# The early shared expert of a two-layer AdaLN kernel: whole blocks of 512 columns in place of halves, and another buffer

## What is computed

```python
h = _layernorm(x) * (1 + cb) + sb          # hidden, 2048 x 128
shared = _silu(hidden @ shared_gate_w.T) * (hidden @ shared_up_w.T) @ shared_down_w.T
x = x + gb * (shared + expert_sum)         # shared_gate_w, shared_up_w: 512 x 128
```

## Time and profile before

| | |
|---|---|
| three runs | 1034.47 to 1039.31 us, median 1035.91 |
| profiled execution | 1037.88 us |
| its span on the core | 1036.2 us |
| TensorE clock granted, mean | 0.959 of full speed |
| steps with the pieces of chunk 0 | about 257 to 374 us of the span |
| steps with the pieces of chunk 1 | about 414 to 531 us of the span |

### The profile page before, as it was taken

One profiled execution on the slowest core, in us unless ns is written; L12 is line 12 of the kernel. 1 busy time (PEld: TensorE's weight loads), 2 busy tenths in 40 slices (PEclk: granted clock), 3 DMA queues, 4 the chain that ended last, 5 costly groups with the idle time before them and its releaser, 6 DMA issues.

```text
span 1036.2 us, 23043 instructions
## 1 busy us (share of the span) xinstructions
PE 955.9 (92%) x9214; PEld 360.0 (35%) x9214; DVE 888.1 (86%) x1321; ACT 810.6 (78%) x1627; POOL 220.6 (21%) x395
## 2 busy tenths in 40 slices
PE   5999999999999999999999889979989998888888
PEld 2552322232333333333333235524323463232224
DVE  7989999999999998999998888854787877899804
ACT  4139999998999998999997678857864576667886
POOL 4233200003221203221112500051132212201112
PEclk9879999999999998999998889989997999999999
DMA  3510400000000000000000164112100441100000
GB/s 103 171 54 2 132 24 10 8 2 2 1 2 2 2 2 2 2 2 2 2 2 1 49 179 132 32 31 73 38 3 1 123 119 36 47 12 2 1 12 11
DMA packets 41387, 37.05 MB, mean 36 GB/s; under 512 B 5084, under 2 KB 39452, under 8 KB 41280
## 3 DMA queue, kind: packets, MB, share of 16 engines
q1 hardware_dynamic: 39024, 30.20, 10.1%
q0 software_dynamic: 1824, 5.25, 1.8%
q10 hardware_dynamic: 432, 0.13, 0.1%
HBM read 21.92 MB, written 13.30 MB: 34 GB/s over the span
## 4 chain that ended last, share of the span: by engine, by line
PE 52%; DVE 31%; issue 7%; ACT 6%; POOL 2%; DMA 1%; another core or an unknown queue 1%; ACTq 0%; POOLq 0%; DVEq 0%; SPq 0%
DVE mx L1374 25%; PE O L1057 19%; PE T L1022 11%; ACT PT L1631 2%; PE T L1136 2%; PE S L995 2%; PE T L1033 2%; PE T L1146 2%; PE S L987 2%; DVE S L1370 1%; ACT PT L1625 1%; PE S L1179 1%; POOL XP L1990 1%; PE O L914 1%; PE S L1128 1%
## 5 line engine op out<-in xcount | busy, mean ns | idle before, releaser
L1374 DVE TENSOR_REDUCE mx<-S 128x2 f32<-128x1024 f32 x608 | 705.7, 1220 | 38.8 <-PE S L987 20.5
L1631 ACT ACTIVATE PT<-T 128x512 f32<-128x512 f32 (+2 forms) x1280 | 657.4, 586 | 99.7 <-PE T L1033 43.2
L1057 PE MATMUL O<-PT,Va 128*9 128x256 f32 (+1 forms) x4040 | 335.5, 393 | 4.5 <-ACT Os L1665 4.5
L1022 PE MATMUL T<-Qs,Ks 26*128 26x512 f16 x1024 | 242.3, 392 | 12.1 <-ACT PT L1631 8.8
L987 PE MATMUL S<-Ks,Qs 24*128 24x512 f16 x1024 | 204.1, 398 | 7.7 <-DVE mx L1374 5.8
L1022 PEld LDWEIGHTS T<-Qs,Ks 26*128 26x128 f16 x1024 | 67.8, 91 | 229.9 <-issue 127.0
L1057 PEld LDWEIGHTS O<-PT,Va 128*9 128x9 f32 x4040 | 67.6, 88 | 125.9 <-issue 112.1
L1057 PE MATMUL O<-PT,V 128*17 128x256 f32 (+2 forms) x984 | 84.6, 414 | 1.4 <-ACT Os L1665 0.7
L995 PE MATMUL S<-K,Qs 48*128 48x512 f16 (+3 forms) x320 | 61.0, 363 | 17.1 <-DVE mx L1374 12.0
L1370 DVE CUSTOM_DVE_ANT_0 S<-S,gates 128x128 f32<-128x128 f32 (+3 forms) x128 | 59.7, 519 | 6.1 <-PE S L995 5.9
L987 PEld LDWEIGHTS S<-Ks,Qs 24*128 24x128 f16 x1024 | 48.2, 91 | 30.9 <-DVE mx L1374 23.7
(11 more groups left out here) (335 smaller groups left out, 894.2 us busy)
## 6 DMA issues: line engine op xcount, KB each, us to landing
Wg<-in_L_ffn_experts SPq DMA_DIRECT2D x28, 192.0 KB, 2.6
Ks<-in_L_ffn_experts SPq DMA_DIRECT2D x20, 192.0 KB, 2.6
Vf<-sorted_x SPq DMA_DIRECT2D x12, 256.0 KB, 4.6
sorted_y<-Vf SPq DMA_DIRECT2D x12, 256.0 KB, 2.3
rows_q<-q SPq DMA_DIRECT2D x7, 256.0 KB, 2.4
sorted_x<-XP POOLq DMA_DIRECT2D x1, 1792.0 KB, 10.7
Qs<-nrow SPq DMA_DIRECT2D x96, 2.0 KB
Qs<-rows_q SPq DMA_DIRECT2D x8, 192.0 KB, 3.7
```

Source lines behind the costliest of these rows:

```text
L1022: e.matmul(bank, Ks[r0:r0 + 26, quad, keys], Qs[r0:r0 + 26, quad, CH * c:CH * c + CH], start=True, stop=True, tile_position=(r0, 0)).then_ ...
L1057: m = e.matmul(acc[32 * g:32 * g + d1, lo:hi], v, PT[(2 * j + g // 2) % 4][:, p0 + lo:p0 + hi], start=fresh, stop=True, skip_group_check=n ...
L1374: e.tensor_reduce(mx[:, u % 2, h0:h0 + 2, kb], two[:, :, 0:n], AX.X, ALU.max).then_inc(free, 1)
L1631: e.activation(PT[(2 * j + pair) % 4][:, CH * i + lo:CH * i + CH], bank[:, lo:CH], ACT.Exp).then_inc(free, 1)
```

## The change

The gate and lift products of chunks 0 and 1 are made for all 512 rows of the chunk at once: 4 gates and 4 lifts for a chunk in place of 8 and 8. The four `lower` pieces stand together at the end in place of two after each half. There are 12 pieces for a chunk in place of 20, and they stand 4.2 steps apart in place of 2.5, so that they cover about the same steps. The buffer `gates` is now 3x512 columns in the last 1536 columns of `Vf`, and `triangle` has a tensor of its own. POOL's product of the second chunk waits for the first chunk's last `lower`.

```diff
@@ -244,10 +244,9 @@
             P.piece[a] = len(P.piece) + 1
             beside("gate", *a)
         pieces = []
-        for half in range(2):
-            for bl in range(4):
-                pieces += [lambda a=(c, bl, half): gate(*a), lambda a=(c, bl, half): beside("lift", *a)]
-            pieces += [lambda j=j: beside("lower", c, j) for j in (2 * half, 2 * half + 1)]
+        for bl in range(4):
+            pieces += [lambda a=(c, bl): gate(*a), lambda a=(c, bl): beside("lift", *a)]
+        pieces += [lambda j=j: beside("lower", c, j) for j in range(4)]
         for i, piece in enumerate(pieces):
             at(s + int(i * apart), piece)
 
@@ -295,7 +294,7 @@
             mix(t, c)
         elif c < 2:
             route(t + 5, c)
-            shared_pieces(t + 10, c, 2.5)
+            shared_pieces(t + 10, c, 4.2)
         elif c == 2:
 
             route(t + 2, 2)
@@ -680,7 +679,6 @@
         onesf = sb("onesf", [128, 128])
         wqT, wkT, wvT, woT = (sb(n, [128, 128]) for n in ("wqT", "wkT", "wvT", "woT"))
         bq, bk, bqs, bks, bv = (sb(n, [128, 1]) for n in ("bq", "bk", "bqs", "bks", "bv"))
-        gates = sb("gates", [128, 3, 256])
         bvb, boB, bpB = (sb(n, [128, 128]) for n in ("bvb", "boB", "bpB"))
         rwT = sb("rwT", [128, 16])
         XP = sb("XP", [128, 16, 128])
@@ -715,6 +713,7 @@
         rk = sb("rk", [128, 208])
         rt = sb("rt", [128, 12, 16])
         lg, eq, wv_ = (rt[:, 4 * i:4 * i + 4, :] for i in range(3))
+        vector_mask = sb("vector_mask", [128, CH], BF16)
         lm = sb("lm", [128, 16])
         wm = sb("wm", [128, 4])
 
@@ -738,7 +737,8 @@
         XS = Vf[:, 0:3584].rearrange("p (i n) -> p i n", n=128)
         ams = [Vf[:, 3584 + CH * i:3584 + CH * i + CH] for i in range(4)]
         bsg, bt = Vf[:, 5632:5632 + CH], Vf[:, 6144:6144 + CH]
-        triangle = gates[:, 0, :].bitcast(BF16)
+        gates = Vf[:, 6656:8192].rearrange("p (k n) -> p k n", k=3)
+        triangle = vector_mask[:, :]
         pick = Vf[:, 0:256].bitcast(F16).rearrange("p (k s m) -> p k s m", k=2, s=2)
         hS, tS, acS = ([Vf[:, 6656 + 512 * k + 256 * i:6656 + 512 * k + 256 * i + 256] for i in range(2)] for k in range(3))
         Kf = Ks[:, :, :].rearrange("p a n -> p (a n)")
@@ -1128,20 +1128,20 @@
                     e.matmul(two[:, 0, :], sgT[:, 128 * bl:128 * bl + 128], hc(c), start=True, stop=True).then_inc(gate_made, 1)
                     e.matmul(two[:, 1, :], suT[:, 128 * bl:128 * bl + 128], hc(c), start=True, stop=True).then_inc(full, 1)
                 elif name in ("gate", "lift"):
-                    c, bl, half = a
+                    c, bl = a
                     done(("turn", 1, c))
                     pe.wait_ge(ld_w1, LD_W1)
-                    bank, full = opened((name, c, bl, half))
+                    bank, full = opened((name, c, bl))
                     w = sgT if name == "gate" else suT
-                    e.matmul(bank[:, 0:256], w[:, 128 * bl:128 * bl + 128], hc(c, 256 * half, 256 * half + 256), start=True, stop=True).then_inc(full, 1)
+                    e.matmul(bank, w[:, 128 * bl:128 * bl + 128], hc(c), start=True, stop=True).then_inc(full, 1)
                 elif name == "lower":
                     c, j = a
                     bank, full = opened(("lower", c, j))
                     pe.wait_ge(po_scaled, SCALED["dn"])
-                    if (c, 3, 0) in P.piece:
-                        pe.wait_ge(gated, P.piece[c, 3, j // 2])
+                    if (c, 3) in P.piece:
+                        pe.wait_ge(gated, P.piece[c, 3])
                     for bl in range(4):
-                        if (c, 3, 0) not in P.piece:
+                        if (c, 3) not in P.piece:
                             done(("up", c, bl))
                         m = e.matmul(bank[:, 0:128], ams[bl][:, 128 * j:128 * j + 128], sdT[:, bl, :], start=bl == 0, stop=bl == 3)
                     m.then_inc(full, 1)
@@ -1710,11 +1710,11 @@
                     bank, free = filled((name,) + tuple(a))
                     if P.piece[tuple(a)] > 1:
                         ac.wait_ge(gated, P.piece[tuple(a)] - 1)
-                    e.activation(gates[:, 0, :], bank[:, 0:256], ACT.Tanh, scale=0.5)
-                    e.activation(gates[:, 1, :], bank[:, 0:256], ACT.Copy).then_inc(free, 1)
+                    e.activation(gates[:, 0, :], bank, ACT.Tanh, scale=0.5)
+                    e.activation(gates[:, 1, :], bank, ACT.Copy).then_inc(free, 1)
                 elif name == "lift":
                     bank, free = filled((name,) + tuple(a))
-                    e.activation(gates[:, 2, :], bank[:, 0:256], ACT.Copy).then_inc(free, 1)
+                    e.activation(gates[:, 2, :], bank, ACT.Copy).then_inc(free, 1)
                 elif name == "m0":
                     g, p = a
                     bank, free = filled(("m0", g, p))
@@ -1965,16 +1965,16 @@
                     po.settle()
                     e.tensor_tensor(hv, hv, sv.unsqueeze(2).to_broadcast([128, 4, 128]), ALU.mult).then_inc(prepared, 1)
                 elif name == "lift":
-                    c, bl, half = a
+                    c, bl = a
                     tanh, gate, lift = (gates[:, i, :] for i in range(3))
-                    done(("lift", c, bl, half))
+                    done(("lift", c, bl))
                     if c:
-                        passed(("lower", c - 1, 2 * half + 1))
+                        passed(("lower", c - 1, 3))
                     po.tick(e.tensor_tensor(tanh, tanh, gate, ALU.mult))
                     po.settle()
                     po.tick(e.tensor_tensor(tanh, tanh, gate, ALU.add))
                     po.settle()
-                    e.tensor_tensor(ams[bl][:, 256 * half:256 * half + 256], tanh, lift, ALU.mult).then_inc(gated, 1)
+                    e.tensor_tensor(ams[bl], tanh, lift, ALU.mult).then_inc(gated, 1)
                 elif name == "scatter":
                     g, t = a
                     po.wait_ge(positions, g + 1)
```

## The result

The changed kernel was slower: a median of 1042.98 us in 9 runs (1035.99 to 1047.91) beside 1034.81 us for the kernel before (1027.35 to 1042.14, 9 runs). The medians are 8.2 us apart. The ratio of the two sets of runs is 1.0092, with a 95% interval of 1.0065 to 1.0119, so 6.7 to 12.3 us more. Forecast was 1042.1 us from a median of 1035.91, that is +6.2. Its profiled execution took 1042.35 us, with a span of 1040.6.

A forecast was written before the change was run, and what follows sets the result against it. DVE was taken to set the pace without slack in layer 0's units; gates, lifts, first gate, collisions and POOL's wait sum to 6.9 us a chunk against 3.8, +6.2 for two, giving 1042.1 us from 1035.91, range 1034 to 1048.

The forecast's parts named there:

- DVE sets the pace: Layer 0 units: DVE has no slack; wide pieces delay its `s` tile, 0.82 us a gate, 0.35 to 0.4 a lift.
- POOL's queue ahead of `neg_turn`: Second lift: longer POOL operations delay the negated maxima's split; PE stands still about 1.5 us, costing 1.2 us a chunk.
- The sum: Units 5 to 7 and the first gate: 6.9 us a chunk in place of 3.8, +3.1; two chunks +6.2.
- the first gate: Gate behind DVE's six routing operations: only PE's longer product counts, 0.35 us a chunk.
- collisions: Units 5 to 7: pieces near `o_turn`, `neg_turn` or each other; 1.3 us a chunk, where narrow ones cost 2.0.
- down projections: Four a chunk, at steps 15, 3, 8 and 13 of a unit: keep their 2.2 us, 0.55 each on average.
- The clock: Units with wide pieces: PE's longer stops lower its clock from 2.4 to 1.2 GHz, time passes 1048 us; 8 in 100.
- Width doesn't matter: Rival: a wide piece costs about its two narrow ones, only POOL's wait remains; 1036 to 1039 us, 34 in 100.
- Instructions count, not columns: Rival: each insertion costs DVE 0.27 us whatever its width, so 16 fewer make it faster; 1030.1 us, 10 in 100.
- The Trainium skill's rule: ACT: two 256-column ACTIVATEs cost 93 ns more than one of 512, saving 2.2 us, off the path where DVE is full.

The follow-up runs named there:

- the kernel with the slower POOL: Kernel before, narrow pieces kept, POOL doing two more 256-column products in one lift per chunk ahead of the negated maxima's split; ratio to before 1.0049 (1.0013 to 1.0085).
- the quarters: Kernel before with pieces of 128 rows: 16 gates and 16 lifts a chunk, 1.35 steps apart, one `lower` per quarter; ratio to before 1.0098 (1.0065 to 1.0131).
- the side work behind the `s` tile: Side work of steps 78 to 191 placed after its half step's `s` tile in PE's order; ratio to before 1.0128 on the changed kernel, 1.0057 on the kernel before.

## Why the prediction was right, and where it was short

- *DVE sets the pace, and the loss is in its gaps.* Shown: 0.88 us at a calm wide gate and 0.39 at a calm wide lift, in DVE's own rows. The sum had 0.82 (2.5 for three) and 0.35 to 0.4, from shifting the narrow gate's rows by 0.4 for PE and 0.42 for ACT; the `s` tile moved by 0.86.
- *POOL's queue ahead of `neg_turn`.* Right in place and size: PE waited 1.71 us where I said 1.5, and it cost 1.5 us a chunk where I said 1.2. Three kernels show it: POOL's order changed took it away, 24 idle products left it, and two more POOL products made 1.2 us of it with narrow pieces.
- *The sum.* Without the low clock, units 5 to 7 of the changed kernel are 118.8 us, 3.1 more than before; in my sum these units had +2.7, and 0.35 for the first gate ahead of them. Taking POOL's wait away leaves 117.3, so the new pieces without it are 1.5 us a chunk above the old ones, where the sum had 5.3 - 3.8 = 1.5. That this is so exact is in part luck: gates, lifts and collisions came to 118.8 - 3 x 36.6 - 1.5 - 1.7 = 5.8, half a microsecond over the sum, and the down projections (below) to as much less. Over the units it was not 39.3 to 40 each: unit 5 has the wait and took 41.5.
- *The clock.* This is what the sum lacked. I had it as a danger of 8 in 100, from PE's longer stops in general, and didn't join it to the one stop that I had worked out. The kernel before had rows for it. In units 4 and 8 PE stands still for 1.05 us, waiting for DVE, and the clock is at its lower level right behind:

```profile
246.10 0.39 PE L987 MATMUL S<-Ks,Qs 24*128 24x512 f16 x2 [1.05 <-DVE mx L1374]
246.42 1.04 PE L1057 MATMUL O<-PT,Va 128*9 128x256 f32 x8
...
403.45 0.61 PE L987 MATMUL S<-Ks,Qs 24*128 24x512 f16 x2 [1.05 <-DVE mx L1374]
```
```profile
403.50:410.30 6.80, 6.80 (x54) 1.47 (x54) 6.06 (x6) 3.55 (x8) 4.09 (x8) 0.50 0.01 2
```

The stop in the forecast, 1.5 us, was longer than these. Where the clock falls behind it for 6.8 us it costs 2.8 us a chunk; for 3.4 us, as in unit 9 of the kernel with the slower POOL, 1.1. The changed kernel's two profiles stand at +5.8 and +3.1 a chunk, 11.6 and 6.2 us in all; the measured interval, 6.7 to 12.3 us, holds the one and begins just above the other.
- *The number.* 1042.1 against 1042.98 looks closer than it was. The forecast was +6.2, the medians are 8.2 us apart, and the interval begins at 6.7: the forecast difference lies a little under it. That the median of the kernel before came out 1.1 us lower in nine runs than in three made up for half of the gap, by luck.
- *Down projections.* I kept their 2.2 us a chunk. In the kernel before DVE's starts at the four are 0.70, 0.50, 0.45 and 0.63 over the pace, 2.3, so the estimate of 0.55 each was right for it. Now they stand alone in unit 7, the first at its edge, and cost 0.34, 0.44, 0.34 and 0.60: 1.7. What was off is that they keep their cost.
- *The rivals.* "Width doesn't matter" falls with the gate's 0.88 against 0.13. "Instructions count, not columns" is wrong for wide pieces, but it holds a part of the truth, which the quarters show: from 256 rows down to 128 a piece gets no cheaper. Narrow pieces hide in what lead PE and ACT have, for a small toll each; a wide one exceeds it and pays nearly in full.
- *The Trainium skill's rule* for an ACTIVATE's fixed cost ("ScalarE: Activation LUTs", section "What ACT_TABLE_LOAD costs") gave 2.2 us less for ACT, an estimate from the page. ACT's busy time fell by 1.2 us with 24 instructions fewer (810.6 to 809.4): the same direction, about half the size. It had no bearing on the time.
- *The rest of the whole time.* Most of it goes with the mean granted clock, which is on record for every execution. Among the 77 executions of the kernel before that stand beside the experiments, 0.001 more of it goes with some 0.7 us less. The quarters were 9.9 us longer on average, over the executions that the ratio compares, at a clock of 0.9525 against 0.9586; at 0.7 us for 0.001 that is 4.3 us of clock, and 5.6 are left, where their units have 4.3. For the side work behind the `s` tile 11.6 - 5.8 = 5.8 us are left with wide pieces and 5.3 - 1.8 = 3.5 with narrow ones, where the units have 5.8 and 4.6. For the changed kernel run again it is 12.2 - 5.5 = 6.7, where its units at full clock have 6.2. These are estimates. By them about half of what the changed kernel lost in that run went with the clock; in which units, the executions without a profile don't show.
- *What stays open.* What decides whether the clock falls behind a stop of PE, and how often it does so in the changed kernel's runs that were not profiled.

## What to carry to other kernels

Where three engines run in step through rings of two and three buffers, ask of each side job how long it holds PE, the bank and the copying engine beyond the lead these have, before counting its instructions: halving the number of pieces made each cost three to seven times as much. And of a side engine that looks idle (POOL, 21% busy) look at what small operation stands next in its queue, and who waits for that one; here moving three of its operations in a chunk gave back 1.5 us a chunk, and took away the stop behind which PE's clock could fall.

## What was not expected of the hardware

A stop of PE of the same length was followed by the low clock or not. Behind 1.71 us the clock was granted at half for 6.8 us in both units of one execution (0.50 in 292.60 to 299.40) and at full in both of another; behind 1.42 us it fell in unit 9 and not in unit 5 of the same execution. With the stop filled by small products, or shortened to 0.40 us, it stayed full in the units that were profiled.

All twelve profiles together say more than one pair. Among their units 5 to 7 and 9 to 11, eight have a stop of PE of 1.4 to 1.8 us, and in four of the eight the clock fell; in the 64 others, whose stops are all under 0.6 us, it never did. Units 4 and 8 have the stop of 1.04 to 1.05 us for DVE in 23 of 24 cases, and in 18 of these the clock fell, at the end of the stop or up to 2.4 us behind it. So in units 4 to 11 a fall always came with a stop, and one of 1 us could do; these counts don't show what else it takes.
